# A Mamba layer and a mixture of experts in one kernel: batch 0's ranking, step-size work and row turns put at other steps

## The chip, the cores and the metric

The kernel runs on one core of one Trainium2 chip. The metric is the device time of one execution in microseconds, given as the median of three runs. Durations of instructions come from one profiled execution and its trace.

## The reference

Eight sequences (batches) of 512 tokens with 128 channels go through two layers side by side, and both results are added to x.

```python
xn = layernorm(x)
# layer 1, Mamba: 256 inner channels, 16 states
xz = (xn * rsqrt(mean(xn * xn) + eps) * norm_w) @ in_proj_w.T
x_s, z = xz[..., :256], xz[..., 256:]
u = silu(causal_conv4(x_s) + conv_b)
x_dbc = u @ x_proj_w.T                      # step size (8), B (16), C (16)
delta = softplus(dt_raw @ dt_proj_w.T + dt_proj_b)
h[t] = exp(delta * A) * h[t-1] + (delta * u) * B[t]      # for each of 16 states
y = sum over states of h * C  + u * D
attn = (y * silu(z)) @ out_proj_w.T + xn
# layer 2, mixture of experts: 8 experts, the best 2 of each token
logits = xn @ w_router.T ; top_w, sel = top_k(logits, 2) ; top_w = softmax(top_w)
ffn = sum over e of gates[:, e] * ((silu(xn @ w_gate[e]) * (xn @ w_up[e])) @ w_down[e])
out = x + attn + ffn
```

## The kernel before

**Steps.** The work is ordered by batch and state: 8 batches of 16 steps, one step for each state of the recurrence. In a step VectorE runs two scans over 512 tokens, one for each half of the 256 inner channels (`scan`, L1129), and multiplies both results by the rows of C (`product`, L1146). TensorE adds the products up over the states (`accumulate`, L1416), ScalarE makes exp(delta * A) for the scans. Everything else is hung into these steps by tests on the step number `k`, in the functions `step0(k)` (batch 0) and `step(b, k)` (batches 1 to 7) of each engine. Each engine runs its own list in the order written and waits on semaphores, so an instruction that waits holds back all that stands behind it on its engine.

**Batch 0.** Its input to the scan, delta * u * B, is made by time: ScalarE scales the turned input (`scaled(k + 2)`, L530, four activations, two steps ahead) and TensorE turns it back into a bank (`dbu_turn(0, k, halves)`, L1379, four transposes for a half). ScalarE then makes the decay of the same state (`decay(k + 2)`, L502, two activations of Exp). `dbu_turn` for the second half of a state stands at the head of TensorE's step, behind all that the step before put there. Both wait for a bank: three banks go round, and half m takes the bank of half m - 3 once its product is done (`freed`). `scaled(k + 2)` in its turn waits until both halves of state k are turned.

**Beside it, in batch 0's steps.** The rows of batches 3 to 7 are turned by `xh_turn` (L1332) and copied by ScalarE (`xh_out`, L473). The router's `logits` (L1338) are multiplied on TensorE. `keep` (L1324) are matmuls whose result nothing reads, on TensorE alone. VectorE picks the two experts of each token at step 7 (`choices`, L1058 to L1068). The ranking of all tokens by expert follows: GpSimd adds the two choices (L860), TensorE counts them (`totals`, L1346), ScalarE copies the counts (`totals_out`, L478), TensorE ranks (`ranking`, L1353 to L1357), ScalarE copies the ranks (`ranks_out`, L483), and GpSimd works out slots and tiles in some 30 small instructions (L869 to L888), whose end (`lohi_rdy`) VectorE's `one_hots` waits for at step 12 (L1088, L1089, L1091: two groups in each of steps 12 to 15). GpSimd's `texp` (L894 to L897), the expert of each tile, ends the ranking.

**Batch 1's step size.** The convolution, x_proj and dt_proj of batch 1 run in batch 0. Softplus is split: `magnitudes` (L740, L741), `vanishing` (Exp, L746), `rounded` (L751), `corrected` (L756) and `logarithm` (Ln, L761) on ScalarE; `raise_sum` (L427), `correct` (L433), `softplus` (L448) and `input_scale` (L456) on GpSimd, each over two halves of 128x512. Ln is in another table than Exp and Tanh, so a table load stands ahead of it and another ahead of the next Exp. `rows(1)` (L1463 on TensorE, L731 on ScalarE) and `steps_mm` (L1471) come first. The convolution of batch 2 (`conv(2, hf, taps)`, L1448) is followed by `half_tanh` (L722, L725) on ScalarE and `unit` (L1160) on VectorE, which comes after the products of its step. The first scans of batch 1 take the decay from `decay_bank(16, hf)` (L514), which waits for batch 1's delta and for a product, and the input from GpSimd (`scaled(16)`, L916). In batch 0 ScalarE ends a step in this order:

```python
                if k in (7, 8):
                    magnitudes(1, k - 7)
                    vanishing(1, k - 7)
                if k == 8:
                    rounded(1)
                    corrected(1)
                    totals_out()
                    logarithm(1)
                    ranks_out()
```

and TensorE's step 8 holds `totals()` and `ranking()` one behind the other, between the turn of state 9's first half and the turn of its second.

## Time and profile before

| what | us |
|---|---|
| median of 3 runs (lowest, highest) | 629.74 (629.36, 631.14) |
| the profiled execution's own time | 628.76 |
| its span | 627.0 |
| mean granted TensorE clock in it | 0.959 of full speed |
| VectorE busy | 590.0 (94%) |
| TensorE busy, its weight loads | 545.1 (87%), 427.4 (68%) |
| GpSimd busy | 509.8 (81%) |
| ScalarE busy | 457.8 (73%) |

Times in the trace count from the start of the span. Batch 0's steps run from 35.3 to 129.5 us; the change lies wholly in them and in the 5 us ahead of them. The column of idle time names the engine and line that ended a wait.

### The profile page before, as it was taken

Reading aid. Unit: us, or ns where it says so; the run is one execution under the profiler, and the core shown is the slowest. Engines: PE = TensorE matmul, PEld = TensorE weight load, DVE = VectorE, ACT = ScalarE, POOL = GpSimd, SP = SyncE. Lnnn points to the kernel's source line nnn. Section 1 sums busy time; section 2 is a strip of 40 time slices with the busy share of each in tenths; the row PEclk is TensorE's granted clock in tenths of the full one; section 3 lists DMA queues with packets and bytes.
Section 4 is the critical chain, followed back from the end, with each engine's and each line's share of the span. In section 5 each row is a group of like instructions: output and inputs, shape, how many; then the busy total and the mean of one; then the engine's idle time right before and its main releaser. Section 6 shows DMA issues by size and latency. Waiting matters only on the chain.

```text
span 627.0 us, 11479 instructions
## 1 busy us (share of the span) xinstructions
PE 545.1 (87%) x3554; PEld 427.4 (68%) x3554; DVE 590.0 (94%) x852; ACT 457.8 (73%) x916; POOL 509.8 (81%) x481
## 2 busy tenths in 40 slices
PE   5999878898898989989899898898989796978887
PEld 2387666656787768877778778787776464757564
DVE  6989969999899998999989999999989998899997
ACT  1798796139866797678876698767985579959881
POOL 5796059459999899998999989998997978875773
PEclk9879888869999999999999999999999999898999
DMA  7420109824867888768868798678894446232364
GB/s 211 137 110 0 72 2 193 287 75 175 284 232 253 261 273 275 270 221 275 282 232 289 247 301 280 214 259 267 281 288 155 147 170 226 93 117 72 100 137 89
DMA packets 60893, 122.99 MB, mean 196 GB/s; under 512 B 8218, under 2 KB 41378, under 8 KB 53794
## 3 DMA queue, kind: packets, MB, share of 16 engines
q1 hardware_dynamic: 53826, 112.42, 52.7%
q0 software_dynamic: 6288, 9.52, 7.3%
q8 instruction: 29, 0.48, 0.3%
q10 hardware_dynamic: 720, 0.33, 0.3%
q14 instruction: 30, 0.25, 0.1%
HBM read 112.77 MB, written 9.47 MB: 195 GB/s over the span
## 4 chain that ended last, share of the span: by engine, by line
PE 45%; DVE 19%; ACT 17%; issue 16%; POOL 1%; DMA 1%; ACTq 0%; DVEq 0%; POOLq 0%
DVE bank L1129 8%; PE bank L1448 8%; PE bank L1416 8%; PE bank L1565 7%; DVE h_sb L1146 6%; PE bank L1579 5%; PE bank L1573 5%; ACT bank L514 3%; PE bank L1471 2%; ACT dbu L530 2%; ACT da L502 2%; PE bank L1379 2%; PE bank L1463 1%; PE bank L1546 1%; ACT th L698 1%
## 5 line engine op out<-in xcount | busy, mean ns | idle before, releaser
L916 POOL TENSOR_TENSOR dbu<-du,xn_all 128x512 f32<-128x512 f32 x172 | 215.3, 1274 | 26.7 <-DVE bank L1129 26.2
L1129 DVE TENSOR_TENSOR_SCAN bank<-bank,dbu 128x512 f32<-128x512 f32 x170 | 206.9, 1219 | 8.9 <-ACT bank L514 8.9
L1146 DVE TENSOR_TENSOR h_sb<-bank,xh_all 128x512 f32<-128x512 f32 x240 | 158.7, 675 | 1.2
L514 ACT ACTIVATE bank<-delta,a_sb 128x512 f32<-128x512 f32 x170 | 116.7, 689 | 53.9 <-DVE h_sb L1146 53.2
L1416 PE MATMUL bank<-id_sb,h_sb 128*128 128x128 f32 x992 | 135.7, 282 | 15.4 <-DVE h_sb L1146 13.0
L1416 PEld LDWEIGHTS bank<-id_sb,h_sb 128*128 128x128 f32 x992 | 116.3, 146 | 26.6 <-DVE h_sb L1146 19.3
L1129 DVE TENSOR_TENSOR_SCAN bank<-da,bank 128x512 f32<-128x512 f32 x82 | 96.5, 1212 | 12.5 <-PE bank L1379 12.4
L1565 PEld LDWEIGHTS bank<-wd_sb,hid 117*128 117x128 f32 (+1 forms) x432 | 55.1, 190 | 58.0 <-DVE hid L1180 33.3
L1565 PE MATMUL bank<-wd_sb,hid 117*128 117x128 f32 (+1 forms) x432 | 63.7, 283 | 28.4 <-ACT xT L687 26.8
L903 POOL DMA_INDIRECT xs<-xn_rows,src x72 | 70.6, 981 | 12.4 <-issue 9.0
L530 ACT ACTIVATE dbu<-du_t,bc_sb 128x256 f32<-128x256 f32 x164 | 69.5, 497 | 12.1 <-PE bank L1379 9.8
L1379 PE MATMUL bank<-id_sb,dbu 128*128 128x128 f32 x328 | 54.4, 292 | 10.9 <-DVE h_sb L1146 9.4
L1448 PE MATMUL bank<-xhT,wk_sb 128*128 128x512 f32 x128 | 62.1, 611 | 0.7 <-ACT xhT L473 0.7
L502 ACT ACTIVATE da<-delta,a_sb 128x512 f32<-128x512 f32 x86 | 58.2, 714 | 5.1 <-DVE bank L1129 5.0
L1379 PEld LDWEIGHTS bank<-id_sb,dbu 128*128 128x128 f32 x328 | 40.7, 151 | 31.0 <-issue 23.6
L1573 PE MATMUL bank<-xT,wgu_sb 128*118 128x128 f32 x432 | 59.2, 273 | 0.2 <-DVE ga L1173 0.2
L1579 PE MATMUL bank<-xT,wgu_sb 128*118 128x128 f32 x432 | 59.0, 272 | 0.0
L965 POOL DMA_INDIRECT xhT<-y_slots,slot x40 | 38.7, 966 | 18.5 <-DVE bank L1129 6.7
L1579 PEld LDWEIGHTS bank<-xT,wgu_sb 128*118 128x118 f32 x432 | 52.7, 181 | 0.5 <-issue 0.5
L1573 PEld LDWEIGHTS bank<-xT,wgu_sb 128*118 128x118 f32 x432 | 52.3, 182 | 0.5 <-issue 0.4
L705 ACT ACTIVATE ys<-bank,stat 128x128 f32<-128x128 f32 x72 | 26.3, 365 | 33.1 <-PE bank L1565 33.0
L698 ACT ACTIVATE th<-bank 118x384 f32<-118x384 f32 x72 | 34.8, 483 | 19.1 <-PE bank L1573 18.4
(197 smaller groups left out, 898.5 us busy)
## 6 DMA issues: line engine op xcount, KB each, us to landing
xh_all<-b_rows SPq DMA_DIRECT2D x30, 1024.0 KB, 7.8
xn_all<-b_rows SPq DMA_DIRECT2D x25, 1024.0 KB, 8.0
wgu_sb<-in_w_gu SPq DMA_DIRECT2D x72, 352.0 KB, 3.6
wd_sb<-in_w_dn SPq DMA_DIRECT2D x72, 192.0 KB, 5.0
y_slots<-ys SPq DMA_DIRECT2D x72, 64.0 KB
xn_rows<-xn_all SPq DMA_DIRECT2D x2, 1040.0 KB, 11.0
out<-x_sb SPq DMA_DIRECT2D x7, 256.0 KB, 7.4
x_sb<-in_x SPq DMA_DIRECT2D x2, 640.0 KB, 6.0
```

What stands on the lines that cost most here:

```text
L502: nc.scalar.activation(da_of(n)[:, hf, :], delta[b % 2][:, hf, :], ACT.Exp, scale=a_sb[:, hf, k:k + 1]).then_inc(s["da_rdy"], 1)
L514: nc.scalar.activation(bank_of(b, m)[:, :], delta[b % 2][:, hf, :], ACT.Exp, scale=a_sb[:, hf, k:k + 1]).then_inc(s["da_rdy"], 1)
L530: last = nc.scalar.activation(dbuT[k % 2][:, t, :], duT[:, t, :], ACT.Copy, scale=bc_sb[q][:, t, k:k + 1])
L916: nc.gpsimd.tensor_tensor(dbu[k % 2][:, hf, :], du[b % 2][:, hf, :], b_ring[c % 2][:, k % CH, :], ALU.mult).then_inc(s["dbu_p"], 1)
L1129: nc.vector.tensor_tensor_scan(at, da_of(n)[:, hf, :] if n in IN_SBUF else at, inp, 0.0, ALU.mult, ALU.add).then_inc(s["h_rdy"], 1)
L1146: nc.vector.tensor_tensor(h_sb[k % 2][:, hf, :], bank_of(b, 2 * k + hf)[:, :], row, ALU.mult).then_inc(s["p_rdy"], 1)
L1379: last = nc.tensor.transpose(at[:, t * P:(t + 1) * P], dbuT[k % 2][:, t, hf * P:(hf + 1) * P], id_sb[:, :])
L1416: last = MM(HT[i][:, t % 2, hf * P:(hf + 1) * P], h_sb[k % 2][:, hf, t * P:(t + 1) * P], id_sb[:, :], is_transpose=True, start=(k == 0 and ...
L1448: last = MM(at[:, :], wk_sb[:, tap, hf * P:(hf + 1) * P], xhT[:, c, tap:tap + T], start=(tap == taps[0] if c == 0 else tap == 0), stop=(ta ...
L1565: last = MM(XD[:, P:P + H], hid[j % 2][0:FN[c], c * P:(c + 1) * P], wd_sb[j % NW][0:FN[c], c, :], start=(c == 0), stop=(c == NF - 1))
L1573: last = MM(GB[0:FW, c * P:(c + 1) * P], wgu_sb[j % NW][:, c * FS:c * FS + FW], xT[j % 2][:, :], start=True, stop=True)
L1579: last = MM(UB[0:FW, c * P:(c + 1) * P], wgu_sb[j % NW][:, F + c * FS:F + c * FS + FW], xT[j % 2][:, :], start=True, stop=True)
```

## The change

On ScalarE the step-size work of batch 1 is spread: `rows(1)` to step 7, `magnitudes` and `vanishing` to steps 8 and 9, `rounded` to 10, `corrected` to 11, `logarithm` to 12; `totals_out` comes between `magnitudes` and `vanishing` of step 8, `ranks_out` and `spread_choices` at the end of step 9. `half_tanh(2, ...)` goes from steps 11 and 14 to 12 and 15, `unit(2, ...)` with it. On TensorE `ranking` goes to step 9, behind `steps_mm(1, 1)`; states 2 and 3 are turned whole, in the step before; one row turn of step 1 goes to a later step, each `logits` moves by a step or so, the three `keep` on the router's bank go; `rows(1)` goes to step 7, `steps_mm` to 8 and 9, the second `skip` to 12, `conv(2, ...)` to 10, 11, 13 and 14. On GpSimd the four pieces of batch 1's softplus go behind `texp`. No arithmetic is added or removed but the `keep`.

```diff
@@ -43,7 +43,7 @@
     NXS = 5
     NW = 4
     ND = 3
-    TURNED, SKIPPED0 = 11, (7, 8)
+    TURNED, SKIPPED0 = 11, (7, 12)
     LN_EPS = 1e-5
     RMS_EPS = float(np.finfo(np.float32).eps)
 
@@ -218,12 +218,12 @@
 
         HOT_STEP = {12: (0, 1), 13: (2, 3), 14: (4, 5), 15: (6, 7)}
         MAP_STEP = {13: (0, 1), 14: (2, 3), 15: (4, 5)}
-        LOGITS_AT = {0: (3,), 3: (4,), 4: (5,), 6: (6, 7)}
+        LOGITS_AT = {0: (2,), 3: (3,), 4: (4,), 5: (5,), 6: (6, 7)}
         LATE_ROWS = {1: (24, 28), 4: (28, 32)}
 
         def b_turn(k):
 
-            return {0: 4, 1: 5, 3: 6, 5: 7}.get(k)
+            return {0: 4, 3: 5, 4: 6, 5: 7}.get(k)
 
         BY_PE = [k for k in range(1, S)] + [6 * S + k for k in (3, 5, 6, 7, 8, 9, 10, 11, 12, 13, 14, 15)] + [7 * S + k for k in range(2, S)]
         BY_POOL = [n for n in range(S, NB * S) if n not in BY_PE]
@@ -555,21 +555,26 @@
                     half_tanh(1, 1)
                 if b_turn(k) is not None:
                     xh_out(b_turn(k))
-                if k == 6:
+                if k == 7:
                     rows(1)
-                if k in (7, 8):
-                    magnitudes(1, k - 7)
-                    vanishing(1, k - 7)
+                if k in (8, 9):
+                    magnitudes(1, k - 8)
                 if k == 8:
+                    totals_out()
+                if k in (8, 9):
+                    vanishing(1, k - 8)
+                if k == 9:
+                    ranks_out()
+                    spread_choices()
+                if k == 10:
                     rounded(1)
+                if k == 11:
                     corrected(1)
-                    totals_out()
+                if k == 12:
+                    half_tanh(2, 0)
                     logarithm(1)
-                    ranks_out()
-                if k == 9:
-                    spread_choices()
-                if k in (11, 14):
-                    half_tanh(2, k // 14)
+                if k == 15:
+                    half_tanh(2, 1)
 
             def step(b, k):
 
@@ -861,8 +866,6 @@
             rt(nc.gpsimd.tensor_tensor(kk[:, :], m2[:, :], m1[:, :], ALU.subtract))
             nc.gpsimd.tensor_tensor(kk[:, :], kk[:, :], irms[:, :], ALU.mult).then_inc(s["top_rdy"], 1)
 
-            for hf in range(NH):
-                raise_sum(pool, nc.gpsimd, 1, hf)
             pool.wait_ge(s["rk_out"], 1)
             pool.wait_ge(s["ones"], 6)
             e0, e1 = [v[:, E:] for v in ends]
@@ -886,15 +889,14 @@
             rt(nc.gpsimd.tensor_scalar(lo[:, :], hi[:, :], -float(P), 0.0, ALU.mult, ALU.add))
             nc.gpsimd.tensor_tensor(lo16[:, :], lo[:, :], slotf[:, :], ALU.add).then_inc(s["lohi_rdy"], 1)
             nc.gpsimd.tensor_copy(hi16[:, :], hi[:, :]).then_inc(s["lohi_rdy"], 1)
-            for hf in range(NH):
-                correct(pool, nc.gpsimd, 1, hf)
-            softplus(pool, nc.gpsimd, 1, 1)
-            input_scale(pool, nc.gpsimd, 1, 1)
             for e in range(E):
                 rt(nc.gpsimd.tensor_scalar(tkey[:, :, e], lanes_sb[0:1, 0:NJ], ends[1][0:1, E + e:E + e + 1], 1.0,
                                            ALU.is_ge, ALU.mult))
             tree(tsum[:, :], tkey, tred4, tred2, ALU.add)
             nc.gpsimd.tensor_scalar(texp[:, 0:NJ], tsum[:, :], float(E - 1), None, ALU.min).then_inc(s["texp_rdy"], 1)
+            remainder(pool, nc.gpsimd, 1)
+            softplus(pool, nc.gpsimd, 1, 1)
+            input_scale(pool, nc.gpsimd, 1, 1)
 
             def load(j):
 
@@ -1203,8 +1205,8 @@
                     unit(1, 1)
                 if k == 7:
                     choices()
-                if k in (11, 14):
-                    unit(2, k // 14)
+                if k in (12, 15):
+                    unit(2, k // 15)
                 if k in z_step(0):
                     z_gate(0, k)
                 if k == 10:
@@ -1581,38 +1583,36 @@
 
             def step0(k):
 
-                if k > 1:
+                if k > 3:
                     dbu_turn(0, k, (1,))
                 if k > 0:
                     accumulate(k - 1)
                 if k + 1 < S:
-                    dbu_turn(0, k + 1, (0, 1) if k == 0 else (0,))
+                    dbu_turn(0, k + 1, (0, 1) if k < 3 else (0,))
                 for g in MAP_STEP.get(k, ()):
                     inverse(g)
                 if k in (1, 2):
                     conv(1, 1, (2 * k - 2, 2 * k - 1))
-                if k == 5:
+                if k == 7:
                     rows(1)
+                if k in (8, 9):
+                    steps_mm(1, k - 8)
                 if k in SKIPPED0:
                     skip(0, (SKIPPED0.index(k),))
                 if k == 8:
                     totals()
+                if k == 9:
                     ranking()
-                if k in (9, 10):
-                    conv(2, 0, (2 * k - 18, 2 * k - 17))
-                if k in (12, 13):
-                    conv(2, 1, (2 * k - 24, 2 * k - 23))
+                if k in (10, 11):
+                    conv(2, 0, (2 * k - 20, 2 * k - 19))
+                if k in (13, 14):
+                    conv(2, 1, (2 * k - 26, 2 * k - 25))
                 if k + 1 in z_step(0):
                     z_mm(0, k)
                 if b_turn(k) is not None:
                     xh_turn(b_turn(k))
                 for i in LOGITS_AT.get(k, ()):
                     logits(i)
-                if k == 7:
-                    steps_mm(1, 0)
-                    steps_mm(1, 1)
-                if k in (0, 4):
-                    keep(LGB[:, 2 * C - 2 * H + 2 * E:])
                 if k >= 12:
                     keep(MAP[:, 2 * NJ:], k == 12)
                     keep(MAP[:, 2 * NJ:], False)
@@ -1703,12 +1703,10 @@
             conv(1, 0, (0,))
             columns(0)
             conv(1, 0, (1, 2, 3))
+            input_turn(0, 0)
             logits(0)
             xh_turn(3)
-            input_turn(0, 0)
             logits(1)
-            logits(2)
-            keep(LGB[:, 2 * C - 2 * H + 2 * E:])
             for k in range(S):
                 step0(k)
             for b in range(1, NB):
```

TensorE, steps 8 and 9 of batch 0, before (L1471 is `steps_mm`, L1379 `dbu_turn`, L1416 `accumulate`, L1428 `skip`, L1346 `totals`, L1353 to L1357 `ranking`):

```order
L1471 MATMUL bank<-bct_full,dtw_sb 128x512 x2
L1379 MATMUL bank<-id_sb,dbu 128x128 x4
L1416 MATMUL bank<-id_sb,h_sb 128x128 x8
L1379 MATMUL bank<-id_sb,dbu 128x128 x4
L1428 MATMUL bank<-dd_sb,u_sb 128x128 x4
L1346 MATMUL bank<-one_sb,sel 128x1 x2
L1353 MATMUL bank<-sel,before_sb 128x256
L1355 MATMUL bank<-tri_sb,totc 128x256 x2
L1357 MATMUL bank<-tri_sb,totc 128x8 x2
L1379 MATMUL bank<-id_sb,dbu 128x128 x4
```

and now (line numbers are 2 higher):

```order
L1473 MATMUL bank<-bct_full,dtw_sb 128x512
L1348 MATMUL bank<-one_sb,sel 128x1 x2
L1381 MATMUL bank<-id_sb,dbu 128x128 x4
L1418 MATMUL bank<-id_sb,h_sb 128x128 x8
L1381 MATMUL bank<-id_sb,dbu 128x128 x4
L1473 MATMUL bank<-bct_full,dtw_sb 128x512
L1355 MATMUL bank<-sel,before_sb 128x256
L1357 MATMUL bank<-tri_sb,totc 128x256 x2
L1359 MATMUL bank<-tri_sb,totc 128x8 x2
L1381 MATMUL bank<-id_sb,dbu 128x128 x4
```

The ranking stood ahead of the turn of state 9's second half; it stands ahead of that of state 10 now, behind one `steps_mm`.

ScalarE, from step 9's end to the last step of batch 0 and the first of batch 1, now (L751 is `vanishing`, L483 `ranks_out`, L530 `scaled`, L502 `decay`, L756 `rounded`, L761 `corrected`, L727 and L730 `half_tanh`, L766 `logarithm`, L669 the gate of batch 0, L514 `decay_bank`):

```order
L530 ACTIVATE dbu<-du_t,bc_sb 128x256 x4
L502 ACTIVATE da<-delta,a_sb 128x512 x2
L727 ACTIVATE u_sb<-bank,cbh_sb 128x512
L730 ACTIVATE u_sb<-u_sb,sign_sb 128x512
L766 ACT_TABLE_LOAD
L766 ACTIVATE sp_d<-sp_d 128x1024
L530 ACTIVATE dbu<-du_t,bc_sb 128x256 x4
L669 ACT_TABLE_LOAD
L669 ACTIVATE zs_sb<-bank 128x512
...
L514 ACTIVATE bank<-delta,a_sb 128x512
L727 ACTIVATE u_sb<-bank,cbh_sb 128x512
L730 ACTIVATE u_sb<-u_sb,sign_sb 128x512
```

The table load and Ln are behind the first `half_tanh` of batch 2 (step 12), and the second `half_tanh` (step 15) is behind `decay_bank(16, 0)`; before, both `half_tanh` stood three and one steps from either.

GpSimd, from the end of the ranking to the first input of batch 1, before (L888 ends `lohi_rdy`, L894 to L897 is `texp`):

```order
L888 CAST hi<-hi 128x64
L433 TENSOR_TENSOR sp_m<-sp_m,sp_e 128x512 x2
L448 TENSOR_TENSOR delta<-sp_d,sp_m 128x512 x2
L456 TENSOR_TENSOR du<-delta,u_sb 128x512 x2
L894 TENSOR_SCALAR wgu_sb<-lanes_sb,ends 1x72 x8
```

and now:

```order
L896 TENSOR_SCALAR texp<-tsum 1x72
L427 TENSOR_TENSOR sp_m<-sp_m,sp_y 128x512 x2
L433 TENSOR_TENSOR sp_m<-sp_m,sp_e 128x512 x2
L448 TENSOR_TENSOR delta<-sp_d,sp_m 128x512 x2
L456 TENSOR_TENSOR du<-delta,u_sb 128x512 x2
L918 TENSOR_TENSOR dbu<-du,xn_all 128x512 x6
```

The eight instructions of the softplus, two of which stood ahead of the ranking, follow each other behind `texp`.

## Rows read from the trace of the kernel before

**Rows 1.** What VectorE waited for in the whole span (us, times, longest)
```profile
DVE bank L1129 <- PE bank L1379: 12.4, 9, 5.0
```
**Rows 2.** VectorE's timeline, batch 0 (start, us, line, operation, [idle before])
```profile
47.13 1.23 DVE L1129 TENSOR_TENSOR_SCAN bank<-da,bank 128x512 f32<-128x512 f32 x1 [1.87 <-PE bank L1379]
49.72 1.23 DVE L1129 TENSOR_TENSOR_SCAN bank<-da,bank 128x512 f32<-128x512 f32 x1 [1.36 <-PE bank L1379]
...
76.86 2.33 DVE L1129 TENSOR_TENSOR_SCAN bank<-da,bank 128x512 f32<-128x512 f32 x2
79.11 1.27 DVE L1146 TENSOR_TENSOR h_sb<-bank,xh_all 128x512 f32<-128x512 f32 x2
...
86.48 1.23 DVE L1129 TENSOR_TENSOR_SCAN bank<-da,bank 128x512 f32<-128x512 f32 x1 [4.97 <-PE bank L1379]
...
98.24 0.75 DVE L1160 SCALAR_TENSOR_TENSOR u_sb<-bank,cb_sb,u_sb 128x512 f32<-128x512 f32 x1 [0.57 <-ACT u_sb L725]
```
**Rows 3.** ScalarE's timeline, step 8
```profile
80.49 1.15 ACT L751 ACTIVATE sp_d<-sp_y,sign_sb 128x1024 f32<-128x1024 f32 x1
...
82.89 1.28 ACT L761 ACT_TABLE_LOAD   x1
```
**Rows 4.** TensorE's timeline, steps 1 and 2
```profile
42.11 1.71 PE L1338 MATMUL bank<-wr_sb,xhT 128*128 128x8 f32 x8
43.67 1.15 PE L1324 MATMUL bank<-wk_sb,id_sb 128*128 128x240 f32 x2
44.61 1.92 PE L1416 MATMUL bank<-id_sb,h_sb 128*128 128x128 f32 x8
46.32 0.70 PE L1379 MATMUL bank<-id_sb,dbu 128*128 128x128 f32 x4
46.86 1.88 PE L1448 MATMUL bank<-xhT,wk_sb 128*128 128x512 f32 x4
```
**Rows 5.** TensorE's timeline, steps 8 and 9
```profile
74.56 1.11 PE L1379 MATMUL bank<-id_sb,dbu 128*128 128x128 f32 x4
75.47 1.91 PE L1416 MATMUL bank<-id_sb,h_sb 128*128 128x128 f32 x8
...
82.93 0.70 PE L1353 MATMUL bank<-sel,before_sb 128*128 128x256 f32 x2 [3.88 <-ACT totc L478]
...
85.28 1.09 PE L1379 MATMUL bank<-id_sb,dbu 128*128 128x128 f32 x4
```
**Rows 6.** Windows: stretch, busy of PE, PEld, DVE, ACT, POOL, granted clock, DMA, GB/s
```profile
42.00:44.00 2.00, 2.00 (x11) 2.00 (x10) 2.00 (x3) 2.00 (x5) 2.00 (x3) 0.50 0.01 4
...
74.00:76.00 2.00, 2.00 (x8) 1.44 (x8) 1.86 (x5) 0.29 (x1) 0.00 (x0) 0.50 0.00 0
```
**Rows 7.** ScalarE's timeline, step 11
```profile
93.95 1.71 ACT L530 ACTIVATE dbu<-du_t,bc_sb 128x256 f32<-128x256 f32 x4 [0.23 <-PE bank L1379]
95.56 1.32 ACT L502 ACTIVATE da<-delta,a_sb 128x512 f32<-128x512 f32 x2
...
97.48 0.72 ACT L725 ACTIVATE u_sb<-u_sb,sign_sb 128x512 f32<-128x512 f32 x1
```
**Rows 8.** VectorE's timeline, the one-hot groups of step 12, and step 13's scans
```profile
102.33 1.66 DVE L1088 TENSOR_TENSOR lo_oh<-lanes_sb,lo 128x1024 f16<-128x1024 f16 x1
...
104.77 0.68 DVE L1088 TENSOR_TENSOR lo_oh<-lanes_sb,lo 128x1024 f16<-128x1024 f16 x1
...
106.23 2.33 DVE L1129 TENSOR_TENSOR_SCAN bank<-da,bank 128x512 f32<-128x512 f32 x2
```
**Rows 9.** GpSimd's timeline, from the ranks to the softplus and texp
```profile
85.95 0.20 POOL L869 TENSOR_SCALAR tiles<-wgu_sb 128x8 f32<-128x8 f32 x1 [4.15 <-ACT wgu_sb L483]
...
95.97 2.50 POOL L433 TENSOR_TENSOR sp_m<-sp_m,sp_e 128x512 f32<-128x512 f32 x2
...
103.41 1.35 POOL L894 TENSOR_SCALAR wgu_sb<-lanes_sb,ends 1x72 f32<-1x72 f32 x1
...
112.75 0.72 POOL L897 TENSOR_SCALAR texp<-tsum 1x72 int32<-1x72 f32 x1
```

## The prediction

> **What bounds the kernel now.** I read the busy times first, then who waited for whom, then the timelines of the four engines over batch 0, and last the granted clock by windows. VectorE is busy 94% of the span, and its largest wait is for TensorE's turns (L1379): 12.4 us in nine waits [rows 1]. So VectorE's list sets the time, and outside batch 0 the change touches nothing. What it can win is the waits in that list, and what it can lose is new waits, or VectorE instructions that become longer. A change counts here only if VectorE reaches batch 1's first scan (129.5 us in this trace) earlier or later; from there all engines shift together.
>
> In batch 0 the reader sees VectorE wait 1.87 and 1.36 us at state 2, 4.97 us at state 9 and 0.57 us at the first `unit(2)` [rows 2]. The 4.97 us have a plain cause: the second half of state 9 is turned at 85.28, behind `ranking`, which could not start before 82.93 because its counts were copied by ScalarE behind `rounded` and `corrected` [rows 5, 3]; a further 0.53 us at state 10 are of the same origin. What the change is made for, then, is 3.2 us at state 2 and 5.5 us at states 9 and 10; with the `unit` that is 9.3 us of waits. 0.3% of the time, 1.9 us, is about what a measurement of this kernel can tell from no change.
>
> **Part 1: states 2 and 3 turned whole.** Before, TensorE ran the logits from 42.11, `keep` from 43.67, `accumulate` from 44.61 and the turn of state 2 from 46.32, then 1.72 us of convolution and a row turn before the second half [rows 4]. Without `keep` (0.94 us) and with the row copy ahead of it 0.3 us earlier, both halves are turned from about 45.1, the first ready at 45.95, the second at 46.6. VectorE, which would be free at about 45.0, waits 1.1 us for the first half and not for the second. State 3 is now behind the convolution (1.72) and `accumulate`: ready at 49.6, wanted at 49.5, so 0.2 us. State 4's second half stands behind a row turn and logits moved to step 3: ready at 54.8, wanted at 54.25, so 0.6 us. Waits of 1.9 in place of 3.2, and 0.3 us from the earlier start: **1.6 us won**. This takes it that the clock, which is low here (0.50) [rows 6], rises at about 46.3 as it did before. The end of the `keep` costs nothing on any path by itself, as nobody reads them; what they cover is the clock. If it rises only behind the convolution, that takes 3.4 instead of 1.7 us, and state 3 is ready at 51.4 instead of 49.6: the 1.6 us are gone (-0.2).
>
> **Part 2: the ranking a step later.** I count from the end of `choices`, when VectorE scans state 8 (76.86). A step is 2.25 us of scans and 1.19 of products [rows 2]. The product of state 8's first half ends at +2.94; TensorE then turns state 9's second half, adds up state 8, turns half of state 10, runs `steps_mm` (1.0 us) and then `ranking`. TensorE has been idle for some 2.8 us ahead of the small `totals` by then, waiting for GpSimd's sum. Before, an idle piece of 1.5 us was followed by the low clock at 74 to 76 us [rows 6], with 0.91 us for four transposes and 1.70 for eight in place of 0.44 and 0.87 [rows 5]. I take the same here: 2.95 + 0.91 + 1.70 + 0.5 = 6.1, + 1.0 for `steps_mm` = 7.1, + 2.35 for `ranking` as measured (82.93 to 85.28 [rows 5]) less some 0.3 for a clock that fell in its midst before = 9.2, + 0.6 for state 10's second half: **+9.8**. VectorE wants it at 3.44 + 3.44 + 1.13 = +8.0, so it waits 1.8 us. ScalarE comes to the same point on its own list (state 11's scaling and decay from +4.0, 2.8 us, `magnitudes` and `vanishing` 1.9, `ranks_out` 0.4, waiting for `steps_mm` between): +9.6. Bounds: 1.1 us at the full clock throughout, 4.3 at the low clock throughout `ranking`.
>
> **Part 3: ScalarE's chain to the two `unit`s.** From +9.8 ScalarE is behind: `scaled` 1.60, `decay` 1.22 and now `rounded` 1.05 in step 10, the same with `corrected` in step 11, then in step 12 `scaled`, `decay` and `half_tanh`, 4.25 as measured in step 11 before (93.95 to 98.20) [rows 3, 7]. That ends at +9.8 + 3.87 + 3.87 + 4.25 = +21.8. VectorE has 2.35 + 1.29 (the router's weights) + 3.44 + 3.44 = 10.5 us to do: +20.3. It waits **1.5 us** at `unit(2, 0)`, where it waited 0.57. The second `half_tanh` is behind `decay_bank(16, 0)` in step 15, which waits for the product of state 15's first half; half an Exp pair (0.66) and the two activations (1.4) with their starts make 2.1 us, in which VectorE has 0.6 us of product: another **1.5 us**, where it waited nothing. The table load (1.28 [rows 3]) and Ln come behind the first `half_tanh`; VectorE has its one-hot groups and the whole of step 13 to do then, so I cost them at 0; without that cover it would be 2.3 us. Waits of parts 2 and 3: 1.8 + 1.5 + 1.5 = 4.8 in place of 4.97 + 0.53 + 0.57 = 6.1, **1.3 us won** of the 5.5. Most of the wait goes from state 9 to state 10 and to the `unit`s.
>
> **Part 4: GpSimd's ten long instructions meet the one-hot groups.** In step 12 `lo_oh` took 1.66 us while GpSimd ran 128x512 TENSOR_TENSORs (until 103.44), and 0.68 once they were over [rows 8, 9]: VectorE's instruction with two SBUF inputs stood until GpSimd's ended. A step's six such instructions take 2.94 us undisturbed, and took 3.90 (102.33 to 106.23) in this one [rows 8]; the other three steps' groups lost 0.7 to 0.8 each. Scans and products read a bank and are not lengthened. GpSimd's chain after the ranks is 85.95 to 95.97, and `texp` 103.41 to 113.47 [rows 9], so with the ranks at +9.7 the slots are ready at +19.8 (wanted at +22.4: no wait) and `texp` ends at about +29.3. Then raise, correct, softplus, scale follow, eight instructions at 1.25 (2.50 for two [rows 9]), and VectorE comes to the groups of step 13 at +29.4. So GpSimd has its whole row of long instructions there, where it had small ones.
>
> How often does VectorE stand? GpSimd's first `texp` instruction, at 103.41, took 1.35 us where later ones took some 0.6 [rows 9]: it stood while `lo_oh` and `hi_val` ran back to back, and got in at the gap ahead of the dependent multiplication. I take that: GpSimd gets in where VectorE waits for its own result, once at the start and twice in the six, 1.2 us each. Step 13: 2.94 + 3.5 = 6.4 in place of 3.8 (+2.6). Step 14 with the rest: 2.94 + 0.3 + 2.4 = 5.6 in place of 3.7 (+1.9). Steps 12 and 15 are free of it: -0.96 - 0.73. **2.8 us lost.** Bounds: if VectorE stood nowhere, 3.3 us would be won; if it stood at every one of the six in step 13, 2.5 us more would be lost.
>
> Batch 1's own inputs are in time: delta's first half at some +36, wanted by `decay_bank` at about +42; the GpSimd input of state 16 ready at +38, wanted at +54. `texp` now ends earlier, so the expert weights are loaded earlier; no wait hangs on that.
>
> **Sum.** -1.6 - 1.3 + 2.8 = -0.1 us on the profiled execution's 628.76. That execution lies 1.0 below the median of the runs shown, 629.74; carried to the median the forecast is **629.6 us, no change**. Its own range is 627.9 to 631.3.
>
> The Trainium skill, SBUF — State Buffer, section "SBUF: two separate sides", says that GpSimd and a VectorE instruction with two SBUF inputs take the port pair they share for the whole instruction, and the other fully blocks. The trace agrees with the blocking (1.66 against 0.68 us), and it speaks against this change. If the pair changed hands at each instruction, the sum would be +2.4 instead of -0.1.
>
> **Rivals.**
> 1. VectorE is not held up by the long row, because it keeps the port through its gaps or GpSimd's row falls between the groups. For it: `lo_oh` and the five behind it ran at full pace beside `texp`. Against: there GpSimd's instructions were short, and at 102.33 one long one held VectorE for a full microsecond. Then -1.6 - 1.3 - 3.3 and about 1.9 for what still collides: 625.4 us. Chance 0.28.
> 2. The clock, the other side: TensorE's idle piece ahead of `totals` leaves the clock low until `ranking` is through. `steps_mm` then takes 1.7 and `ranking` 3.3 to 4.4, state 10 is turned at +12.3 in place of +9.8, and everything on ScalarE's chain follows: 632.1 us. It decides from the point where the clock is still low at +7. For it: 42 to 44 us stayed at 0.50 with TensorE busy all the time [rows 6]. Against: right behind that stretch the convolution took 1.88 us, the pace of the full clock [rows 4], and TensorE has the turns and `accumulate` to do ahead of `ranking`. Chance 0.14.
> 3. Port held at every instruction of the group: 632.1 us, with GpSimd's eight used up in step 13. For it: the page named above; against: `texp`'s first instruction was passed by two of VectorE's. Chance 0.15.
>
> **How the numbers follow.** The forecast has 0.43, of which 0.04 each lie beyond 1.9 us on either side. Faster by over 0.3% (below 627.9): 0.28 + 0.04 = 0.32. Slower (above 631.6): 0.14 + 0.15 less the part of these two that stays under it, and 0.04: 0.27. Within: 0.41. The range takes in most of the rivals: 625.6 to 632.3.
>
> **What would show it.** Right, if VectorE's wait for L1379 at state 9 is gone and one of 1 to 3 us stands at state 10; if `unit` (L1162 now) waits about 1.5 us twice; if L1090 and L1091 of step 13 have instructions of 1.5 us and more beside GpSimd's L427 to L456; if state 2's waits fall to about 1 us. The windows between 77 and 84 us show the clock. Wrong, if the groups of step 13 take under 4 us (rival 1), if L1355 starts after +8.5 (rival 2), or if a wait for L514 or for GpSimd's input stands at batch 1's first scans, for which I see no reason.

## The result and the profile after

The change makes the kernel **slower by 0.7%**: 633.01 us (median of 7) beside 629.74 (median of 7), ratio 1.0070, 95% interval 1.0047 to 1.0094. Two later measurements of the same two kernels gave 1.0063 (1.0043 to 1.0083) and 1.0068 (1.0045 to 1.0091). The forecast was 629.6, no change; 633.01 lies above its range of 625.6 to 632.3.

The profiled execution took 632.45 us (span 630.6). The code below the change has moved by two lines: the scan is L1131, the product L1148, `unit` L1162, the turn L1381. VectorE's waits in the whole span (us, times, longest), against [rows 1]:

```profile
DVE bank L1131 <- PE bank L1381: 7.8, 7, 2.4
DVE u_sb L1162 <- ACT u_sb L730: 2.6, 2, 1.5
```

The wait for turns fell from 12.4 to 7.8 us, and the two `unit`s wait 2.6 us together where they waited 0.57. VectorE's timeline of batch 0, against [rows 2, 8]:

```profile
54.86 2.83 DVE L1051 TENSOR_SCALAR xh_all<-x_sb,mean,both 128x128 f32<-128x128 f32 x4
...
85.33 1.23 DVE L1131 TENSOR_TENSOR_SCAN bank<-da,bank 128x512 f32<-128x512 f32 x1 [2.36 <-PE bank L1381]
...
97.55 0.75 DVE L1162 SCALAR_TENSOR_TENSOR u_sb<-bank,cb_sb,u_sb 128x512 f32<-128x512 f32 x1 [1.09 <-ACT u_sb L730]
...
105.20 0.78 DVE L1090 TENSOR_TENSOR lo_oh<-lanes_sb,lo 128x1024 f16<-128x1024 f16 x1
105.90 1.52 DVE L1091 TENSOR_TENSOR hi_val<-lanes_sb,hi 128x576 f16<-128x576 f16 x1
107.46 1.42 DVE L1093 TENSOR_TENSOR hi_val<-hi_val,lanes_sb 128x576 f16<-128x576 f16 x1
108.80 1.77 DVE L1090 TENSOR_TENSOR lo_oh<-lanes_sb,lo 128x1024 f16<-128x1024 f16 x1
110.49 1.54 DVE L1091 TENSOR_TENSOR hi_val<-lanes_sb,hi 128x576 f16<-128x576 f16 x1
112.06 1.40 DVE L1093 TENSOR_TENSOR hi_val<-hi_val,lanes_sb 128x576 f16<-128x576 f16 x1
113.38 2.33 DVE L1131 TENSOR_TENSOR_SCAN bank<-da,bank 128x512 f32<-128x512 f32 x2
```

and GpSimd's beside it, against [rows 9] (two instructions in a row of the first four):

```profile
104.16 2.95 POOL L427 TENSOR_TENSOR sp_m<-sp_m,sp_y 128x512 f32<-128x512 f32 x2
107.07 2.94 POOL L433 TENSOR_TENSOR sp_m<-sp_m,sp_e 128x512 f32<-128x512 f32 x2
109.97 3.18 POOL L448 TENSOR_TENSOR delta<-sp_d,sp_m 128x512 f32<-128x512 f32 x2
113.11 2.73 POOL L456 TENSOR_TENSOR du<-delta,u_sb 128x512 f32<-128x512 f32 x2
```

The 4.97 us at state 9 are gone, 2.36 stand at state 10. The groups of step 13 take 8.18 us (105.20 to 113.38) where they took 3.78: from the second instruction on, each stands behind one of GpSimd's. GpSimd's pairs are stretched as well, from 2.50 to between 2.73 and 3.18. The four steps' groups take 18.4 us together, 15.1 before.

That does not yet explain the result. Batch 1's first scan comes at 130.32, only 0.78 us later than before, while the span is 3.6 us longer. The other 2.8 us arise in batches 6 and 7, whose code and work are unchanged. So the first question was whether one trace of each is a fair pair. In the traces that follow, a granted clock of 1.00 is TensorE's upper level (2.4 GHz) and 0.50 its lower one (1.2 GHz).

### The profile page after: what moved, and what is told of

Its sections match the earlier page's. It is cut to its first block, busy times and chain, and to the rows that moved or that the text cites. A ratio compares the mean times of both kernels' runs of the same rounds, so it can differ in the third digit from the quotient of the medians.

```text
span 630.6 us, 11465 instructions
## 1 busy us (share of the span) xinstructions
PE 540.3 (86%) x3548; PEld 422.4 (67%) x3548; DVE 595.7 (94%) x852; ACT 456.9 (72%) x916; POOL 511.0 (81%) x481
## 4 chain that ended last, share of the span: by engine, by line
PE 39%; DVE 29%; issue 18%; ACT 12%; DMA 1%; POOL 0%; DVEq 0%; ACTq 0%
DVE bank L1131 12%; DVE h_sb L1148 8%; PE bank L1418 7%; PE bank L1567 7%; PE bank L1450 5%; PE bank L1581 5%; PE bank L1575 4%; PE bank L1381 2%; PE bank L1473 2%; ACT bank L514 2%; PE bank L1465 1%; PE bank L1548 1%; ACT dbu L530 1%; ACT L514 1%; DVE lo_oh L1090 1%
## 5 line engine op out<-in xcount | busy, mean ns | idle before, releaser
L1131 DVE TENSOR_TENSOR_SCAN bank<-bank,dbu 128x512 f32<-128x512 f32 x170 | 207.9, 1225 | 8.9 <-ACT bank L514 8.9
L1148 DVE TENSOR_TENSOR h_sb<-bank,xh_all 128x512 f32<-128x512 f32 x240 | 160.0, 681 | 1.2
L514 ACT ACTIVATE bank<-delta,a_sb 128x512 f32<-128x512 f32 x170 | 116.8, 689 | 50.8 <-DVE h_sb L1148 48.4
L1418 PE MATMUL bank<-id_sb,h_sb 128*128 128x128 f32 x992 | 133.1, 278 | 15.4 <-DVE h_sb L1148 13.0
L1418 PEld LDWEIGHTS bank<-id_sb,h_sb 128*128 128x128 f32 x992 | 114.4, 144 | 26.6 <-DVE h_sb L1148 18.4
L1131 DVE TENSOR_TENSOR_SCAN bank<-da,bank 128x512 f32<-128x512 f32 x82 | 96.6, 1214 | 9.9 <-PE bank L1381 7.8
L905 POOL DMA_INDIRECT xs<-xn_rows,src x72 | 70.6, 981 | 12.4 <-issue 9.1
L530 ACT ACTIVATE dbu<-du_t,bc_sb 128x256 f32<-128x256 f32 x164 | 69.5, 497 | 11.1 <-PE bank L1381 7.2
L1381 PE MATMUL bank<-id_sb,dbu 128*128 128x128 f32 x328 | 53.7, 290 | 16.3 <-DVE h_sb L1148 13.9
L1450 PE MATMUL bank<-xhT,wk_sb 128*128 128x512 f32 x128 | 64.8, 634 | 0.7 <-ACT xhT L473 0.7
L502 ACT ACTIVATE da<-delta,a_sb 128x512 f32<-128x512 f32 x86 | 58.3, 714 | 6.8 <-DVE bank L1131 4.7
L1381 PEld LDWEIGHTS bank<-id_sb,dbu 128*128 128x128 f32 x328 | 39.9, 149 | 34.5 <-issue 26.9
```

The costliest lines, as they stand in the source:

```text
L514: nc.scalar.activation(bank_of(b, m)[:, :], delta[b % 2][:, hf, :], ACT.Exp, scale=a_sb[:, hf, k:k + 1]).then_inc(s["da_rdy"], 1)
L530: last = nc.scalar.activation(dbuT[k % 2][:, t, :], duT[:, t, :], ACT.Copy, scale=bc_sb[q][:, t, k:k + 1])
L905: nc.gpsimd.indirect_dma_start(xs[i][:, :], None, xn_rows, bass.IndirectOffsetOnAxis(ap=src[:, j:j + 1], axis=0)).then_inc(s[f"xs_in{i}"], 16)
L1131: nc.vector.tensor_tensor_scan(at, da_of(n)[:, hf, :] if n in IN_SBUF else at, inp, 0.0, ALU.mult, ALU.add).then_inc(s["h_rdy"], 1)
L1148: nc.vector.tensor_tensor(h_sb[k % 2][:, hf, :], bank_of(b, 2 * k + hf)[:, :], row, ALU.mult).then_inc(s["p_rdy"], 1)
L1381: last = nc.tensor.transpose(at[:, t * P:(t + 1) * P], dbuT[k % 2][:, t, hf * P:(hf + 1) * P], id_sb[:, :])
```

## The experiments

The table is read from each kernel's trace. "Wait" is VectorE's at states 9 and 10, with the granted clock while `ranking` ran ("low" is 0.50 to 0.56, "full" 1.00, "mixed" 0.73). "Groups" are the one-hot groups of steps 12 to 15 together. "Start" is batch 1's first scan, "rest" the stretch from there to the first g_sb at the end (before: 129.54 to 621.40). "Ratio" is to the kernel before, timed beside it; it is not the quotient of the two medians, and where the two speak differently the text gives both.

| kernel | wait, clock | groups | start | rest | median | ratio (interval) |
|---|---|---|---|---|---|---|
| before | 5.5, mixed | 15.1 | 129.54 | 491.9 | 629.74 | |
| r_before | 6.1, low | 15.3 | 130.64 | 491.7 | 629.08 | 1.0008 (0.9988 to 1.0029) |
| after | 2.4, full | 18.4 | 130.32 | 494.8 | 633.01 | 1.0070 (1.0047 to 1.0094) |
| r_after | 4.9, low | 19.0 | 133.22 | 491.7 | 632.29 | 1.0063 (1.0043 to 1.0083) |
| r_after2 | 3.8, low | 18.4 | 133.26 | 491.5 | 632.03 | 1.0068 (1.0045 to 1.0091) |
| e1 early | 4.8, low | 15.7 | 126.84 | 493.8 | 629.08 | 0.9997 (0.9976 to 1.0018) |
| e2 order | 4.7, low | 16.2 | 131.72 | 493.8 | 630.03 | 1.0006 (0.9985 to 1.0027) |
| e3 tanh | 2.1, full | 19.1 | 130.05 | 495.4 | 632.77 | 1.0046 (1.0022 to 1.0071) |
| e4 short | 2.3, full | 17.2 | 128.74 | 494.4 | 631.45 | 1.0036 (1.0015 to 1.0056) |
| e5 late | 2.4, full | 18.3 | 130.68 | 492.0 | 630.15 | 1.0044 (1.0028 to 1.0060) |
| e6 order | 4.9, low | 16.1 | 130.76 | 491.3 | 629.71 | 1.0039 (1.0023 to 1.0056) |
| e7 order, tanh | 3.8, low | 16.1 | 129.72 | 491.9 | 628.66 | 1.0009 (0.9994 to 1.0024) |
| e8 keep | 2.6, full | 18.4 | 132.12 | 492.2 | 631.33 | 1.0033 (1.0008 to 1.0057) |
| e10 order, keep | 1.2, full | 18.0 | 129.54 | 491.9 | 629.00 | 1.0017 (0.9994 to 1.0039) |
| e9 all three | 0.5, full | 18.1 | 126.40 | 490.5 | 626.62 | 0.9978 (0.9955 to 1.0000) |
| e12 fenced | 2.1, full | 13.9 | 125.06 | 494.3 | 629.63 | 0.9996 (0.9978 to 1.0015) |
| e11 fenced all | 1.2, full | 15.5 | 123.98 | 494.5 | 626.41 | 0.9953 (0.9928 to 0.9978) |
| e13 e11 less early | 0.5, full | 15.5 | 126.48 | 493.7 | 627.01 | 0.9947 (0.9925 to 0.9969) |
| e15 free | 4.9, low | 12.5 | 126.49 | 491.3 | 625.21 | 0.9971 (0.9946 to 0.9996) |
| e14 free all | 1.2, full | 12.6 | 121.58 | 494.8 | 624.94 | 0.9957 (0.9936 to 0.9979) |

Apart from the first pair the rows form five sets, each measured on one chip: e1 to e4; e5, e6, e7 and r_before; e8, e9, e10 and r_after; e11 to e13; e14, e15 and r_after2. The second and the third set are from the same chip, the others from three more. The kernel before took 629.8, 627.9, 628.3, 629.7 and 628.0 us in them. Medians of different sets are compared by their ratios.

**e1_early**: the kernel before with the early part alone (states 2 and 3 turned whole, `b_turn`, `LOGITS_AT`, the order ahead of the steps, and the three `keep` gone; all of it on TensorE and in the row copies).

> Only the early part of the change on the kernel before (states 2 and 3 turned whole, row turns, logits and the input turn moved, the three keep gone). In the changed kernel the choices ended 1.95 us earlier than before (74.91 against 76.86), so if that part stands alone batch 1's first scan starts at about 127.6 in place of 129.5 and the kernel takes 627.8 us, 2 us less than before. The changed kernel also lost 2.8 us behind batch 5, in stretches where only VectorE stood. Theory A, that loss comes from how TensorE's instruction stream was shortened (the keep): then it shows here too and the time is 629 to 631. Theory B, it comes from the later part (ranking and step-size work): then nothing of it shows here.

629.08 us, ratio 0.9997, not the 627.8 expected. Its trace ended `choices` 2.8 us earlier than before's, but that profiled execution was the fastest of its ten; in the median at most 0.7 us were won. Its rest of 493.8 looked like theory A; the rests of the later sets speak against it (below).

**e5_late_only**: the late part alone.

> The kernel after with states 2 and 3 turned by halves again, `keep` and the row copies at their old places: the late part of the change alone. In the first batch: the waits at the first states are back (3.2 us), state 10 waits some 2.4 us, the two units 1.1 and 1.5, the groups of steps 12 to 15 take 3.0, 8.2, 4.3 and 2.9 us (18.4 in place of 15.1). Theory (collision, what the early part wins stays won): batch 1's first scan at 129.54 - 1.1 + 3.2 = 131.6, 2 us later than before, and the time some 632 to 633, as slow as after or slower. Rival (the early part is what costs, through the lower clock or the later instruction loads it leaves behind): the time is below after's by 1.5 us or more. Rival (the tail of the program costs 2 to 3 us in every kernel whose first batch is not timed as before's was): batches 6 and 7 take as long as in after, from the first scan of batch 1 to the last g_sb 494 us or more, against 491.9 in the profile of before.

630.15 us, ratio 1.0044 (1.0028 to 1.0060), less than after's 1.0063 to 1.0070. So the late part alone costs 2.8 us (1.8 to 3.8), and the early part did not visibly win anything back on top of it (the intervals overlap). And its waits at the first states were gone, though the old order was back: the clock was at 1.00 there. Two rows of windows, of e5 and of r_after (which has the new order):

```profile
42.00:44.00 2.00, 2.00 (x13) 1.48 (x12) 2.00 (x6) 2.00 (x5) 2.00 (x4) 1.00 0.00 0
```
```profile
42.00:44.00 2.00, 2.00 (x11) 2.00 (x12) 2.00 (x6) 2.00 (x5) 2.00 (x4) 0.50 0.00 0
```

So the place where the clock is low changes from one execution to the next, and with it the waits at the first states: 0.4 us in e5 and 4.4 in r_before with the old order, 0.4 in after and 2.0 in r_after with the new one (states 1 to 4).

There is also a floor. VectorE's next stop is `rows_normed` of step 4. In the kernels that come to it early it stands beside GpSimd's row of 128x512 TENSOR_TENSORs of 1.18 us (seven of them from 48.79 to 56.84 in after): 2.83 us in place of 1.11. The `unit` behind it starts at 57.2 to 58.6 in all 16 traces with the early part. It starts at 57.45 in e5 without that part and with the full clock, at 59.96, 60.28 and 60.11 in the three traces without it and with the low clock (both of before, and e13). Up to this place the early part wins 1.4 to 2.9 us when the clock is low at 42 us in both, and nothing when it is full in both.

**e4_short_pool**: `raise_sum` and `correct` of batch 1 on 8 of 512 columns; this leaves out most of batch 1's rounding correction of softplus.

```diff
-                nc.gpsimd.tensor_tensor(sp_m[:, hf, :], sp_m[:, hf, :], sp_y[:, hf, :], ALU.add)
+                nc.gpsimd.tensor_tensor(sp_m[:, hf, 0:8], sp_m[:, hf, 0:8], sp_y[:, hf, 0:8], ALU.add)
```

> The changed kernel with raise_sum and correct of batch 1 run on 8 of 512 columns (this leaves out most of the rounding correction of batch 1's step size). It takes away the work of four of GpSimd's eight long instructions and nothing else, so it prices the collision: by the port theory the groups of step 13 take some 4 to 5 us in place of 8.2, and batch 1 starts 3 to 4 us earlier than in the changed kernel (126.5 to 127.5), time 629 to 630. If the groups were slow for another reason, they stay at 8 us.

631.45 us, ratio 1.0036: 1.7 to 2.1 us less than after by the ratios, and not the 629 to 630 expected. Softplus and scale moved up into the space and met the groups in the place of the others: step 13 still took 7.02 us, and batch 1 started at 128.74, later than the 126.5 to 127.5 expected.

**e2_pool_order, e6_full_order**: raises ahead of the ranks, and the correction (e6: softplus and scale too) ahead of `texp`.

```diff
+            for hf in range(NH):
+                raise_sum(pool, nc.gpsimd, 1, hf)
             pool.wait_ge(s["rk_out"], 1)
...
+            for hf in range(NH):
+                correct(pool, nc.gpsimd, 1, hf)
             for e in range(E):
```

> The changed kernel, with GpSimd's raise_sum ahead of the ranking and correct ahead of texp; softplus and scale stay behind texp. Port theory (VectorE's one-hot groups of step 13 stand behind GpSimd's long TENSOR_TENSORs one by one): four of the eight leave that stretch, texp ends some 1.3 to 2.5 us later, the groups of steps 12 to 15 take 15 us together in place of 18.4, and batch 1's first scan starts near 127, 3 us earlier; time about 630. Rival (ScalarE's chain and the clock are what counts): raise_sum delays the ranks' use by about 1 us, nothing is won, 633 to 634.

> The kernel after with GpSimd's eight long pieces at other places: the two raises ahead of the ranks, correction, softplus and scale between the slots and texp. Same work. Theory (collision by port): GpSimd runs texp, whose instructions are short, when VectorE comes to the groups of step 13, so these take 3.0 to 3.5 us in place of 8.2 and step 14's 3.0 in place of 4.3; some of the long pieces may meet step 12's (up to +1.5). Batch 1's first scan comes 4 to 6 us before after's (130.32), the time is 627 to 628.5. Rival (the groups are long for another cause than GpSimd's long pieces): they stay above 6 us. Rival (what is won in the first batch is given back in batches 6 and 7): batch 1's first scan at 125 to 126, but the time no better than 629.5.

630.03 and 629.71 us, ratios 1.0006 and 1.0039. Both traces missed the start that was expected (131.72 for 127, 130.76 for 124 to 126), and e6 the time of 627 to 628.5. In e6 step 13's groups fell from 8.2 to 2.9 us, as expected, but step 12's rose from 3.0 to 5.0 and step 14's from 4.3 to 5.2: the collision had moved. And state 10 waited 4.7 to 4.9 us. That was not this order's doing, as r_after showed later.

**e3_tanh_first, e7_order_tanh**: `half_tanh(2, 1)` ahead of `decay_bank(16, 0)` in ScalarE's step 15; e7 with e6's order.

> The changed kernel, with the second half_tanh of batch 2 ahead of decay_bank(16, 0) in step 15. The wait of unit(2, 1), 1.53 us in the changed kernel, goes, and decay_bank is still in time behind it, so batch 1 starts 1.5 us earlier: 631.5 us. If the wait was not on the path (GpSimd's second input of batch 1 sets the start), nothing changes.

> The same with half_tanh(2, 1) ahead of decay_bank(16, 0) in ScalarE's step 15. By the profile of the run that had this alone, the wait of 1.5 us at the second unit is gone and batch 1 pays some 0.9 of it back for its decay that comes later: 0.6 us under the same order without it. If the first batch alone counted: 1.5 us under it. If batch 1 takes all of it back: no difference.

The 1.5 us at the second `unit` are gone in both. e3 took 632.77 us (ratio 1.0046), not 631.5: its trace gave 2.0 us back in batch 1. e7 took 628.66: 1.0 us under e6 by the medians, between the two values expected, and 1.9 by the ratios (1.0009 against 1.0039).

**r_before, r_after**: both kernels once more.

> The kernel before once more, for a second trace of it and as a measure of what two equal kernels differ by: ratio 1.000 within 0.003. Theory on the tail (a stall of some 2 us in which VectorE alone stands, near 527 to 531 us, that comes and goes by chance): it may stand here too, and the stretch from batch 1's first scan to the last g_sb is 491.9 to 494.5. Rival (before's instruction stream does not have it): the stretch is 491.9 again within 0.3.

> The kernel after once more, beside the kernel before on this chip. If the first measurement holds, 1.005 to 1.009. Two readings of the state-10 wait: if the clock's fall meets ranking in some executions and not in others, this profile may show 2.4 or 4 to 5 us, and the eight or so times spread over 2 us or more. Batches 6 and 7: if their extra 2 to 3 us belong to the chip or the moment and not to the kernel, the stretch from batch 1's first scan to the last g_sb is the same here as in the three kernels above within 0.5 us, long or short; if they belong to the kernel after, it is 494.8 here and 491.9 in e9 and e10.

r_after and r_before ran on one chip and make a fairer pair than the first two traces: start 133.22 against 130.64, and equal rests. In r_after state 10 waits 4.87 us, not 2.36. TensorE's timeline of r_after around `ranking` (L1355 to L1359):

```profile
75.72 0.60 PE L1348 MATMUL bank<-one_sb,sel 128*128 128x1 f32 x4 [0.70 <-POOL sel L865]
77.84 1.09 PE L1381 MATMUL bank<-id_sb,dbu 128*128 128x128 f32 x4 [1.51 <-DVE h_sb L1148]
...
81.42 2.07 PE L1473 MATMUL bank<-bct_full,dtw_sb 8*128 8x512 f32 x2
83.42 1.22 PE L1355 MATMUL bank<-sel,before_sb 128*128 128x256 f32 x2
84.44 1.91 PE L1357 MATMUL bank<-tri_sb,totc 128*128 128x256 f32 x4
86.14 0.86 PE L1359 MATMUL bank<-tri_sb,totc 128*128 128x8 f32 x4
```

and the same of after:

```profile
75.84 1.01 PE L1348 MATMUL bank<-one_sb,sel 128*128 128x1 f32 x4 [1.70 <-POOL sel L865]
...
82.83 0.70 PE L1355 MATMUL bank<-sel,before_sb 128*128 128x256 f32 x2
83.36 1.03 PE L1357 MATMUL bank<-tri_sb,totc 128*128 128x256 f32 x4
84.23 0.51 PE L1359 MATMUL bank<-tri_sb,totc 128*128 128x8 f32 x4
```

The granted clock, last column but two, of after and then of r_after:

```profile
80.00:82.00 2.00, 2.00 (x9) 1.67 (x8) 2.00 (x4) 2.00 (x4) 0.00 (x0) 0.50 0.00 0
82.00:84.00 2.00, 2.00 (x7) 1.09 (x7) 0.97 (x1) 1.09 (x3) 0.00 (x0) 0.99 0.04 8
```
```profile
82.00:84.00 2.00, 2.00 (x3) 0.50 (x2) 0.85 (x1) 0.47 (x1) 0.00 (x0) 0.50 0.04 8
84.00:86.00 2.00, 2.00 (x6) 1.63 (x5) 0.00 (x0) 1.43 (x3) 0.00 (x0) 0.50 0.00 0
```

In both, TensorE has idle pieces around `totals`, and the clock falls. In after it fell in the window 74 to 76 us (0.81) and is back at 82, in time for `ranking`; in r_after it fell from 76 to 78 us (0.72) and stays low through it. Of the eleven traces that have TensorE's and ScalarE's steps 8 and 9 as in after, six show the low clock in `ranking` (3.8 to 4.9 us of wait) and five the full one (2.1 to 2.4). Of after's own three traces, two show the low one.

The rests settle the other question. They are 491.3 to 492.2 us for seven of the eight kernels of the second and third set and for e15 and r_after2, and 493.7 to 495.4 for all seven of the first and fourth. e9 has 490.5; e14 has 494.8, but loses 3.2 us in batch 1 and not in batches 6 and 7. VectorE's timelines of after and r_after in batch 6:

```profile
529.31 2.34 DVE L1131 TENSOR_TENSOR_SCAN bank<-da,bank 128x512 f32<-128x512 f32 x2 [1.98 <-PE bank L1381]
```
```profile
535.16 0.69 DVE L1249 SCALAR_TENSOR_TENSOR zs_sb<-zs_sb,bank 128x512 f32<-128x512 f32 x1 [1.44 <-ACT zs_sb L669]
```

The stall of 1.98 stands in the eight traces with a long rest, but where it stands the 1.44 at the other place are missing, so the exchange costs little. The greater part arises in batch 7, where after has a second stall and r_after has none:

```profile
589.47 1.23 DVE L1131 TENSOR_TENSOR_SCAN bank<-da,bank 128x512 f32<-128x512 f32 x1 [2.23 <-PE bank L1381]
```

From the end of batch 6 to the end of batch 7 (g_sb to g_sb) the eight traces take 57.2 to 58.4 us and the twelve others 55.7 to 56.0. The same kernel after has both stalls in one measurement and neither in two others, so they aren't the change's. In after the turns to which they are put down were done at 527.5 and 588.0, and the granted clock was 1.00 at both. What makes them was not found; the sets differ in chip and in moment, and these experiments cannot part the two.

**e8_keep, e10_order_keep, e9_all**: TensorE kept busy in step 8. e10 has e6's order besides, e9 also `half_tanh` first.

```diff
                 if k == 8:
+                    for i in range(3):
+                        keep(XHB[:, 0:3 * P], i == 0)
                     totals()
+                    for i in range(2):
+                        keep(XHB[:, 0:3 * P], False)
```

> The kernel after with five `keep` matmuls of 384 columns, whose result nobody reads, in TensorE's two idle pieces of step 8 (1.70 us ahead of totals, 1.11 us behind it): three ahead of totals, two behind. In the profiles so far the clock falls in that stretch in every run, and ranking runs at the full clock in some (state 10 waits 2.05 to 2.4 us: after, e3, e4, e5) and at the low one in others (3.8 to 4.9: e2, e6, e7, of both GpSimd orders only the one with raise_sum ahead of the ranks). Theory (the idle pieces let the clock fall): the windows from 74 to 86 us show 0.9 to 1.0, state 10 waits 1.0 to 1.5 us, and the time is 1 to 2.5 us under after's. Rival (the clock falls whatever TensorE does there): 2 us or more of wait as before, and the keeps only lengthen the stretch. Rival for the order (raise_sum ahead of the ranks delays the ranks themselves, by GpSimd's queue): then this run says nothing on it, and e10 shows state 10 waiting 3.5 us or more at the full clock.

> e6_full_order (GpSimd's eight long pieces away from the groups of step 13) with the same five `keep`. Clock theory: state 10 waits 1.0 to 1.5 us here too, batch 1's first scan comes 4.5 to 5.5 us before that of e8 (collision gone, all else equal) and the time is 4 to 5.5 us under e8's. Rival (collision is given back elsewhere): the difference in time is under 2 us though batch 1 starts 4 us earlier.

> The same with half_tanh(2, 1) ahead of decay_bank(16, 0) as well: by e3's profile 0.6 us under e10, by the first batch alone 1.5 us under it. This is the version that is to beat both kernels: 624 to 625.5 us beside a before of 628 to 629.7, a ratio of 0.993.

The clock stays at 1.00 through steps 8 and 9 in all three, as this row of e8 shows, and state 10 waits 0.5 to 1.2 us. In e8 another 1.4 us stand at state 9, whose second half is turned behind the last two `keep`; no other kernel with them shows this.

```profile
82.00:84.00 2.00, 2.00 (x14) 1.32 (x12) 1.94 (x3) 2.00 (x5) 0.00 (x0) 1.00 0.03 8
```

In the time the keeps are worth 1.0 us by the medians (e8 against r_after) and 1.9 by the ratios; 1 to 2.5 were expected. e10 against e8 gave 2.3 us (1.0 by the ratios) where I expected 4 to 5.5. VectorE, held less at state 10, came to the groups of step 12 3.2 us earlier than in e6 (97.78), and GpSimd's correction only 1.3 us earlier (96.28). So the correction reached into them as well: step 12 took 7.9 us, and the four groups 18.0 beside e8's 18.4. e9 took 626.62, ratio 0.9978 (0.9955 to 1.0000), where 624 to 625.5 and 0.993 were expected.

**e12_fenced, e11_fenced_all, e13_fenced_noearly**: the long pieces released by the end of a group.

```diff
             for e in range(E):
+                if e == 4:
+                    pool.wait_ge(s["hi_rdy"], 2)
+                    for hf in range(NH):
+                        correct(pool, nc.gpsimd, 1, hf)
+                    softplus(pool, nc.gpsimd, 1, 1, (0,))
...
+            pool.wait_ge(s["hi_rdy"], 4)
+            softplus(pool, nc.gpsimd, 1, 1, (1,))
+            input_scale(pool, nc.gpsimd, 1, 1, (0,))
+            pool.wait_ge(s["hi_rdy"], 6)
+            input_scale(pool, nc.gpsimd, 1, 1, (1,))
```

> The kernel after with GpSimd's order alone changed, now so that no long piece can meet a one-hot group: the raises ahead of the ranks; correction and the first softplus half released by the end of step 12's groups (in the middle of texp), the second softplus half and the first scale by the end of step 13's, the last scale by the end of step 14's. e6 and e10 only moved the collision to step 12 (5.0 and 7.9 us there), so they priced it badly. Theory: the four groups take 3.0 us each, some 12 in place of 18.4, batch 1's first scan comes 6 us earlier than in a profile of after with the same state-10 wait, and the time is 5 to 6.5 us under after's: a ratio of 0.996 to 0.999 to before. Rival (given back later): groups at 12 us, but the time less than 3 us under after's.

> e9_all (keeps in step 8's idle pieces, half_tanh(2, 1) first) with the same releases. The groups take 12 us in place of e9's 18, batch 1's first scan comes 5.5 us before e9's 126.4, the time is 5 us under e9's: some 621.5 beside a before of 628.3, a ratio of 0.989. If the collision were worth only what e10 showed against e8 (2.3 us, of a collision that had only moved), the time stays above 624.

> e11 without the early part (states 2 and 3 turned by halves, `keep` in steps 0 and 4 back). By my prediction the early part is worth 1.6 us. The profiles so far: where the clock is low at 40 to 46 us, before's order waits 4.3 to 4.4 us at the first states and after's 1.6 to 2.7; where it is at the full level, 0.7 (e5) against 0.7 (after). So this should be slower than e11 by a value between 0 and 2.4 us, depending on how often the clock is low there. Rival, from e5 against after (the late part alone was 0.2% faster than both parts): the early part costs time, e13 is faster than e11.

e12's ratio is 0.9996 where after's is 1.0063 to 1.0070: about 4.4 us less, for groups that are 4.5 us shorter, where 5 to 6.5 had been expected for groups of 12 us. Step 14 still collided (4.95 us), as `texp` ended at 110.8, when the groups began, and softplus followed it. e11 took 626.41, ratio 0.9953. I had expected 621.5 beside a before of 628.3, which is 622.9 beside this set's 629.7; its groups took 15.5 us and not 12. e13 took 0.6 us more than e11 by the medians and 0.4 us less by the ratios, within the intervals: the early part is worth little.

**e15_free, e14_free_all, r_after2**: two pieces put further up into `texp`, and the scaling of state 17 behind the last group.

> e12 with its three remaining meetings taken away: the second softplus half and the first scale are released by the end of step 13's groups in the middle of texp (in e12 they waited for texp's end and met step 14's groups, 4.95 us), and the scaling of state 17 waits for the end of step 15's groups. The kernel after in all else. Theory: the four groups take 2.9 to 3.0 us each, 12 in place of 13.9 in e12 and 18.4 in after; the time is 6 to 6.5 us under after's measured beside it (e12: some 4.4 under). Rival: what is won in the groups beyond e12 is given back to the units or to batch 1's first states, and the time is e12's within 0.5 us.

> The same on e11 (keeps in step 8, half_tanh(2, 1) first): groups 12 us in place of 15.5 there, batch 1's first scan 3.5 us before e11's 123.98 with the same early waits, time some 3 us under e11's: a ratio to before of 0.990 to 0.992. Rival as above: no better than e11's 0.995.

> The kernel after beside both, on the same chip: 1.005 to 1.008 to before. If the time that e15 saves against it is 6 us or more, the collision (groups at 18.4 in place of 12) is the larger part of what after lost; if it is under 4, it is not.

e15 took 625.21 us beside 632.03 for after on the same chip: **6.8 us less**, 6.1 by the ratios. Its batch 1 starts 6.8 us earlier than r_after2's: 5.9 by the groups (12.5 in place of 18.4), about 1.5 by shorter waits at the first states and state 7, less 1.1 at state 10; 0.4 us of it are not accounted for. The rests are equal (491.3 and 491.5). So the whole collision's price is some 6 us, and it is kept to the end; before's groups at 15.1 paid some 2.6 of it already. Step 13 in its trace:

```profile
107.19 0.69 DVE L1101 TENSOR_TENSOR lo_oh<-lanes_sb,lo 128x1024 f16<-128x1024 f16 x1
107.79 0.50 DVE L1102 TENSOR_TENSOR hi_val<-lanes_sb,hi 128x576 f16<-128x576 f16 x1
...
110.21 2.33 DVE L1142 TENSOR_TENSOR_SCAN bank<-da,bank 128x512 f32<-128x512 f32 x2
```

The expectation for e15 was 6 to 6.5. e14 is the fastest, 624.94, ratio 0.9957, but only 0.3 us better than e15 and not the 0.990 to 0.992 expected. Its batch 1 starts 4.9 us before e15's, and 3.4 are given back behind that; the first of its new waits, which e15 does not have:

```profile
141.48 0.56 DVE L1185 SCALAR_TENSOR_TENSOR ga<-th,bank 118x384 f32<-118x384 f32 x1 [1.06 <-ACT th L702]
143.03 1.23 DVE L1141 TENSOR_TENSOR_SCAN bank<-bank,dbu 128x512 f32<-128x512 f32 x1 [0.39 <-ACT bank L514]
```

## Why the prediction was wrong

The collision that Part 4 named is real and is the largest cost. What the sum had wrong were above all the two gains it was set against. The halves of the change show it in the time: the late part alone, for which the sum had +1.5 us (-1.3 + 2.8), cost 2.8 (e5), and the early part, for which it had -1.6, won 0.2 by its ratio (e1).

- **Part 1 (1.6 us won).** I took the low clock of [rows 6] as fixed in place. It is a matter of the single execution. With the low clock the first states wait 4.3 to 4.4 us in the old order and 2.0 and 2.6 in r_after and r_after2; VectorE comes to step 4's `unit` 1.4 to 2.9 us earlier in the new one. (The 3.2 us of the prediction left out 1.04 us at state 1, which went with them.) With the full clock both orders are held by GpSimd's instructions until 57.2 or later, and the gain is 0. In the times: e1 0.2 us by its ratio; e13 against e11 0.6 by the medians and -0.4 by the ratios; e5 against after some 1.4 the other way. A gain of 1.6 us is seen in none. The low clock at 42 us stood in three of the four traces with the old order, so its absence in some executions is not shown to be the whole reason.
- **A wait put at nothing.** The prediction looked at the clock around 42 and 77 us only. Moving `rows(1)` from step 5 to 7 leaves TensorE idle there: before, it ran `rows(1)` at 60.76; in all 17 traces with the late part it stands 1.6 to 3.3 us ahead of the next turn. Behind that the clock is at 0.50 for some microseconds, and state 7, which waited nothing in before, r_before and e1, waits 1.1 to 1.5 us in five of the 17 and 0.3 to 0.4 in six. The rows of r_after2, TensorE's, its clock's and VectorE's:

```profile
61.95 0.63 PE L1381 MATMUL bank<-id_sb,dbu 128*128 128x128 f32 x4 [1.60 <-DVE h_sb L1148]
```
```profile
66.00:68.00 2.00, 2.00 (x11) 2.00 (x12) 1.57 (x2) 0.00 (x0) 0.00 (x0) 0.50 0.00 0
```
```profile
68.72 1.23 DVE L1131 TENSOR_TENSOR_SCAN bank<-da,bank 128x512 f32<-128x512 f32 x1 [1.15 <-PE bank L1381]
```

- **Part 2 (1.8 us at state 10).** With the clock back in time the wait is 2.1 to 2.4: `choices` end at 74.91, the scan comes at +10.4 where I said +9.8. But the assumption of the step that the clock is back before `steps_mm` failed in six of eleven traces. Then `steps_mm` takes 2.07, `ranking` 3.3 to 3.6, and state 10 waits 3.8 to 4.9 us, where the step had 1.8. That is rival 2, to which I gave 0.14 as if it were one case for all executions; two of after's three traces show it, and in r_after L1355 starts at +8.64, past the +8.5 that the prediction named as its sign (in r_after2 at +7.92, with the clock low all the same). Before's own `ranking` is exposed to the same fall, but for less: 5.5 and 6.1 us of wait in its two traces.
- **Part 3 (1.5 and 1.5 us).** 1.09 and 1.53. The table load behind the first `half_tanh` cost nothing, as costed.
- **Part 4 (2.8 us lost).** Lost are 3.3 us (18.4 against 15.1), 3.7 in the pair r_after and r_before. The working was off in its rule. I had GpSimd get in three times, once at the start and twice in the six instructions, 6.4 us for step 13. It gets in ahead of every one from the second on, 8.18, as rival 3 said. Step 14 took 4.28 and not 5.6, because the pieces were used up sooner. The two errors nearly cancel, which was luck. (Part 4's heading says ten long instructions; the row has the eight that its text counts.) What the prediction cites from the Trainium skill's page SBUF — State Buffer, section "SBUF: two separate sides", that one side's instruction has the shared ports whole while the other blocks, agrees with the trace on VectorE's side: its instruction of 0.45 us takes 1.4 to 1.55, about one of GpSimd's 1.25 more. GpSimd's are stretched by 0.1 to 0.3 us each, less than the VectorE instruction let in between. The alternative worked out beside it, that the pair changes hands at each instruction, is what the trace shows.

In the pair r_before and r_after, from one chip, the sum reads: first states -2.4 (4.42 to 1.98), states 9 and 10 -1.2 (6.05 to 4.87), `unit`s +2.1 (0.52 to 2.61), groups +3.7 (15.3 to 19.0). That makes +2.1, where batch 1's first scan is 2.6 us later and the span 2.6 us longer. Parts 2 and 3 together, for which I had 1.3 us won, are 0.9 lost; with the low clock in `ranking` that is the term whose sign failed. In the first pair, with the full clock in after's, they are 1.1 won. How much of the remaining 0.7 to 1.5 us up to the medians' 3.3 to 4.1 comes from the early part's gain being absent in some executions, and how much from state 7's wait, was not measured by itself.

The 2.8 us by which batches 6 and 7 of the first two traces differ are no part of it: both kernels have rests of 491.7 in their second traces.

## What to carry to other kernels

Before a long GpSimd row is moved beside VectorE instructions that read both inputs from SBUF, count each of those at about one GpSimd instruction more (1.0 us more each here, for a GpSimd instruction of 1.25); and if the row must run there, release it by the end of VectorE's group, as e15 does: that turned a loss of 0.7% into a gain of 0.3% (interval 0.04 to 0.5%). Moving work off TensorE leaves a gap where it stood; a stretch in which TensorE idles ahead of critical work is to be costed at both clocks, with a share of the executions for each, since one trace shows only one. Two traces of the same kernel are worth more than a closer reading of one: they would have shown that 2.8 of the 3.6 us between the first pair had nothing to do with the change.

## What the runs showed of the hardware

- VectorE's 128x576 f16 TENSOR_TENSOR takes 0.45 us alone and 1.4 to 1.55 beside a row of 128x512 f32 TENSOR_TENSORs on GpSimd; that row goes from 1.25 to some 1.5 us an instruction. Even the four instructions of `rows_normed`, TENSOR_SCALARs with one large input, took 2.83 in place of 1.11 us together while GpSimd ran its row of 1.18 us TENSOR_TENSORs. GpSimd's small 1x72 instructions of `texp` beside the groups cost VectorE 0.1 us or so each time (0.50 for 0.45 in e15), and one of 1x288 cost 0.6 (1.05 for 0.45 in before).
- The granted clock falls in the same stretches of the program, behind idle pieces of TensorE (0.7 to 1.7 us around `totals`, 1.6 to 3.3 us at step 5 where `rows(1)` left it), but at a point that differs between executions of one kernel (around `totals` in the window 74 to 76 us in after, 76 to 78 in r_after, 80 to 82 in r_after2), and so does its return. Five matmuls of 384 columns in the pieces around `totals` kept it at 1.00 from 76 to 86 us in all six traces that have them.
- VectorE stood 2.0 to 2.1 us near 523 to 531 us, and 1.0 to 2.2 us again near 583 to 590 us, in all seven kernels of two sets and in the first trace of after, and in none of the twelve other traces; in after nothing in the trace accounts for either. The second makes the most of the difference: batch 7 takes 57.2 to 58.4 us with it and 55.7 to 56.0 without.
